# One step of a fused graph-convolution, Mamba and LSTM block: the order of three additions on GpSimd and two activations on ScalarE

## What is computed

```python
h = relu(adj @ layernorm(x) @ gcn_w + gcn_b); h = layernorm(h) * ln_g + ln_b
xz = h @ w_in;  u = silu(conv4(xz[:, :256]) + conv_b);  z = xz[:, 256:]
dbc = u @ w_xp
dt = softplus(dbc[:, :8] @ w_dt + b_dt)          # this line is what the change touches
B, C = dbc[:, 8:24], dbc[:, 24:40]
state[n] = exp(dt * A[n]) * state[n] + dt * B[n] * u      # 16 states n, scan over 8192 tokens
y = sum_n(C[n] * state[n]) + u * D_skip
x1 = x + (y * silu(z)) @ w_out
out = x1 + lstm_part(layernorm(x1))
```

## Time and profile before

| | |
|---|---|
| runs, median of 3 (lowest, highest) | 1579.28 us (1578.86, 1580.91) |
| profiled execution, its own time | 1580.11 us |
| its span in the profile | 1578.3 us |
| TensorE matmul busy | 1504.4 us, 95% |
| VectorE busy | 1360.7 us, 86% |
| GpSimd busy | 1134.1 us, 72% |
| ScalarE busy | 1025.7 us, 65% |
| granted TensorE clock, mean | 0.986 |

### The profile page before, as it was taken

How to read it: one execution, slowest core, us unless ns; L and a number is a source line. 1 busy time by engine, 2 the same in 40 slices (tenths; PEclk the granted TensorE clock), 3 DMA queues, 4 the chain that set the end, 5 groups by cost and what they waited for, 6 DMA issues and landing times. The chain is left out here.

```text
span 1578.3 us, 17939 instructions
## 1 busy us (share of the span) xinstructions
PE 1504.4 (95%) x4976; PEld 768.4 (49%) x4976; DVE 1360.7 (86%) x1617; ACT 1025.7 (65%) x2180; POOL 1134.1 (72%) x542
## 2 busy tenths in 40 slices
PE   7999999999999999999999999999997789999995
PEld 3444434444444444444444444444442235999994
DVE  7405999999999999999999999999999897667998
ACT  3254757666666767676767585757666755777774
POOL 0325989898989898989898898989898883000223
PEclk9999999999999999999999999999998899999998
DMA  9877767777777777676767777777752523000002
GB/s 364 336 244 275 256 230 243 246 252 243 257 244 259 244 238 263 233 260 240 244 238 259 243 249 254 248 252 248 252 190 73 181 74 118 16 0 1 0 0 107
DMA packets 65404, 322.46 MB, mean 204 GB/s; under 512 B 7036, under 2 KB 7088, under 8 KB 32437
## 3 DMA queue, kind: packets, MB, share of 16 engines
q1 hardware_dynamic: 54433, 302.21, 55.0%
q10 hardware_dynamic: 10900, 19.44, 4.2%
HBM read 309.27 MB, written 12.35 MB: 204 GB/s over the span
## 5 line engine op out<-in xcount | busy, mean ns | idle before, releaser
L655 PE MATMUL bank<-ring,xh 128*128 128x512 f32 x2048 | 956.7, 594 | 10.9 <-DVE xh L1296 8.1
L1428 DVE TENSOR_TENSOR_SCAN work<-bank,hstate,work 128x512 f32<-128x512 f32 x512 | 628.8, 1272 | 20.3 <-ACT bank L965 13.0
L655 PEld LDWEIGHTS bank<-ring,xh 128*128 128x128 f32 x2048 | 387.6, 190 | 462.6 <-issue 422.5
L1159 POOL TENSOR_TENSOR work<-work 128x1024 f32<-128x1024 f32 x210 | 495.8, 2361 | 85.5 <-DVE work L1369 77.1
L965 ACT ACTIVATE bank<-work,a_neg 128x512 f32<-128x512 f32 x512 | 344.6, 686 | 250.5 <-DVE work L1428 247.1
L1361 DVE TENSOR_TENSOR work<-work,bank 128x1024 f32<-128x1024 f32 x253 | 307.1, 1219 | 62.2 <-POOL work L1135 54.4
L1369 DVE TENSOR_TENSOR work<-work,bank 128x1024 f32<-128x1024 f32 x168 | 201.8, 1201 | 23.3 <-POOL work L1159 23.3
L541 PE MATMUL bank<-bc_parts,sel 96*128 96x512 bf16 x422 | 161.8, 384 | 23.5 <-DVE work L1361 22.6
L1245 POOL TENSOR_TENSOR work<-work 128x256 f32 x32 | 27.3, 854 | 213.2 <-ACT work L1032 213.2
L536 PE MATMUL bank<-work,w_sb 128*128 128x512 f32 (+2 forms) x352 | 175.3, 594 | 1.3 <-issue 0.8
L1104 POOL TENSOR_TENSOR work<-work 128x1024 f32<-128x1024 f32 x48 | 113.7, 2369 | 18.5 <-ACT work L839 18.4
(11 more groups left out here) (163 smaller groups left out, 1589.7 us busy)
## 6 DMA issues: line engine op xcount, KB each, us to landing
ring<-adj_t SPq DMA_DIRECT2D x256, 1024.0 KB, 5.4
xh<-c_scratch SPq DMA_DIRECT2D x34, 256.0 KB, 3.3
work<-c_scratch ACTq DMA_DIRECT2D x28, 256.0 KB, 5.9
c_two<-c_scratch ACTq DMA_DIRECT2D x28, 256.0 KB, 5.0
xh<-x_rows SPq DMA_DIRECT2D x16, 256.0 KB, 7.2
work<-x_t SPq DMA_DIRECT2D x16, 256.0 KB, 5.3
x_scratch<-work ACTq DMA_DIRECT2D x16, 256.0 KB, 3.6
work<-x_scratch SPq DMA_DIRECT2D x1, 4096.0 KB, 14.6
```

The lines of the kernel that those rows point to most:

```text
L655: last = nc.tensor.matmul(mixed[:, :], xn[:, j, :], a, start=(j == 0), stop=(j == BLK - 1))
L1159: nc.gpsimd.tensor_tensor(out=acc, in0=hc[0] if n == 1 else acc, in1=hc[n % 2], op=ALU.add).then_inc(y_added, 1)
L1428: nc.vector.tensor_tensor_scan(hb[s % 2][:, h, :], da[h], (dbu_late[POOL_DBU.index(s)] if on_pool else dbu[s % 2])[:, h, :], hstate[:, HV ...
```

## The change

On ScalarE the last two of the four activations change places: (1 + e) - 1 now comes third, into wd, and the logarithm fourth, into wc. On GpSimd the first addition is now relu + e, which needs only e. It stands where the remainder stood. Then comes add(11), and only behind it (1 + e) - 1 is taken off, in the new function take_rem. "Low" now waits for that, and no more for add(11). dt is then that result plus the logarithm. In step 16 the first addition goes one slot earlier (slot 11 of the plan, program slot 12), and take_rem stands in slot 12 of the plan. Step 1 has no scan, so both stand together there.

```diff
                         act.wait_ge(one_dt, k)
-                        nc.scalar.activation(wd, wc, ACT.Ln).then_inc(log_dt, 1)
-                        act.wait_ge(log_dt, k)
-                        nc.scalar.activation(wc, wc, ACT.Identity, bias=less_one[:, :]).then_inc(less_dt, 1)
+                        nc.scalar.activation(wd, wc, ACT.Identity, bias=less_one[:, :]).then_inc(less_dt, 1)
+                        act.wait_ge(less_dt, k)
+                        nc.scalar.activation(wc, wc, ACT.Ln).then_inc(log_dt, 1)
...
-                    if s == 12:
-
-                        pool.wait_ge(less_dt, k)
-                        nc.gpsimd.tensor_tensor(out=wb, in0=wc, in1=wb, op=ALU.subtract).then_inc(rem_dt, 1)
+                    if s == (11 if drains(k) else 12):
+
                         pool.wait_ge(pos_dt, HV * k)
-                        pool.wait_ge(rem_dt, k)
-                        nc.gpsimd.tensor_tensor(out=wa, in0=wa, in1=wb, op=ALU.subtract).then_inc(sum_dt, 1)
+                        pool.wait_ge(exp_dt, k)
+                        nc.gpsimd.tensor_tensor(out=wa, in0=wa, in1=wb, op=ALU.add).then_inc(sum_dt, 1)
+                    if s == 12 and not (scan and not drains(k)):
+                        take_rem()
                     if s == 13:
                         pool.wait_ge(mid_rounded, k)
-                        if drains(k):
+                        if scan and drains(k):
                             pool.wait_ge(pool_hc_done, hc_count(cs, 13, True))
-                        elif scan:
-                            pool.wait_ge(y_added, (DS - 1) * cs + 11)
                         else:
-                            pool.wait_ge(sum_dt, k)
+                            pool.wait_ge(rem_dt, k)
...
-                        pool.wait_ge(sum_dt, k)
+                        pool.wait_ge(rem_dt, k)
                         pool.wait_ge(log_dt, k)
-                        nc.gpsimd.tensor_tensor(out=dt[q], in0=wa, in1=wd, op=ALU.add).then_inc(dt_ready, 1)
+                        nc.gpsimd.tensor_tensor(out=dt[q], in0=wa, in1=wc, op=ALU.add).then_inc(dt_ready, 1)
+
+                def take_rem():
+
+                    pool.wait_ge(less_dt, k)
+                    pool.wait_ge(sum_dt, k)
+                    nc.gpsimd.tensor_tensor(out=wa, in0=wa, in1=wd, op=ALU.subtract).then_inc(rem_dt, 1)
...
                     elif scan and s >= 2:
                         add(s - 1)
+                        if pre and s == 12:
+                            take_rem()
```

## The result

The kernel after takes 1592.94 us, median of 4 runs (1591.9 to 1594.93); the kernel before, run beside it, 1580.1 us (4 runs, 1578.86 to 1581.81). The ratio is 1.0076 (95% interval 1.0064 to 1.0088), and the difference 12.8 us. The forecast was 1591.2 us, 11.9 us more than before, in a range of 1586.0 to 1595.5. The profiled execution of the kernel after took 1593.57 us with a span of 1591.7 us, 13.4 us more than the span before; the granted clock is 0.986 of full speed in both. One execution of the kernel before, of the 16 timed beside e5 to e7, took 5588.44 us; it counts as slow and is left out of the ratios there.

What follows compares the result with a forecast made beforehand. Bound: a ring of waits between VectorE and GpSimd, 75.23 us a step, with one through TensorE's `out` close under it. Terms 12.3 + 1.1 - 1.5 = +11.9 us on 1579.28 gave 1591.2 us, range 1586.0 to 1595.5.

Steps and rivals of the forecast that it cites:

- The wait at add(11): GpSimd, scanning steps: add(11) comes one instruction earlier and waits 1.11 us for VectorE's product hc(11).
- The new period: Steps 3 to 15, hc(15) to hc(15): 76.18 us against 75.23, +12.3 us in all.
- VectorE's wait at hc(15): Sign in the profile after: VectorE's wait before hc(15) up from 1.7 to about 2.6 us.
- TensorE's at the spread: Sign in the profile after: TensorE's wait at the spread up from 0.8 to about 1.75 us.
- The 6.0 us that the transfers might have given back: TensorE's weight load waiting for adj data: at most 13 x 0.46 = 6.0 us back, not taken into the forecast.
- Step 2: Scanning step without `out` yet: hc(15) at 210.71 instead of 209.65, +1.1 us.
- Step 1: Step without a scan: earlier relu + e, but the next scan is released by ScalarE's exponential; 0.
- the second ring: hc(15), dbu, TensorE's spread to `out`, hc(11): 59.44 us, slack before; closing, it makes every step pay.
- The rival that the wait is paid once: Steps 3 to 15: TensorE slack between spread and `out` absorbs the delay, no change, 1577.6 us; chance 0.08.
- ScalarE's exchange of two activations: ScalarE's chain of four: same total length, logarithm about 1 us later but covered; cost nothing.
- Step 16, "-1.5 us": GpSimd: first addition falls into its gap behind hc(11), dtu comes 1.56 us earlier; -1.5 us.
- a rival, 1592.7 us: Step 16's gain is lost, held up by TensorE or step 17's loads: 1592.7 us, inside the range; no separate chance.

Runs made afterwards that it cites:

- e5: Kernel after with the subtraction ahead of add(11) again in steps before 16, and dtu behind add(13) in the full steps: 1565.3 us, ratio 0.9897.
- e7: Kernel before with only the new formula and the exchanged activations, additions in their old places in step 16 too: 1580.57 us, ratio 0.9997.
- e1: Kernel after with the subtraction ahead of add(11) again in all scanning steps, step 16 as changed: 1577.15 us, ratio 0.998.
- e2: Kernel after with TensorE's `out` in slot 11 instead of 11.5, not in the drains: 1594.86 us, ratio 1.0092.
- e11: Kernel after with two of TensorE's adjacency products left out in slot 9 of each scanning step up to 15: 1576.93 us, ratio 0.9976.
- e10: Kernel after with GpSimd's hc(0) of step 16 waiting for VectorE's addition of the skip product: 1591.7 us, ratio 1.0061.
- e8: Kernel after with two of TensorE's adjacency products left out in slot 5 of each scanning step up to 15: 1597.33 us, ratio 1.011.
- e9: Kernel before with two of TensorE's adjacency products left out in slot 5 of each scanning step up to 15: 1582.43 us, ratio 1.0006.
- e12: Kernel before with two of TensorE's adjacency products left out in slot 9 of each scanning step up to 15: 1582.94 us, ratio 1.0013.

## Why the prediction was right, and where it was not

**The wait at add(11): right.** Forecast 1.11 us, measured 0.80 to 1.24 us over the 14 steps, and e1 without it loses nothing.

**The new period: right, 76.15 against 76.18 us**, and with it +11.9 against +12.3 us for steps 3 to 15. VectorE's wait at hc(15) came to 2.62 us, TensorE's at the spread to 1.74, VectorE's for `out` stayed at 1.03, as stated. The 6.0 us that the transfers might have given back did not come: from hc(15) to hc(11) it is still 59.50 us in step 7.

**Step 2: right**, +1.05 against +1.1 us. **Step 1** was put at 0; its stretch came 0.42 us earlier, which isn't more than executions differ by.

**Why the second ring closes: the right ring and length, but a wrong link.** The prediction had hc(11) hang on `out`, and took the rest of the way to it as VectorE's own work. In between VectorE's scan waits 0.30 us for ScalarE, and that wait is the one that counts: the ring leaves TensorE at dt's product and goes through ScalarE's activations of the softplus. e2 took `out` out of the way and nothing moved; e11 shortened the queue ahead of dt's product, and the wait at add(11) vanished. The forecast came out because the 59.44 us from hc(15) to hc(11) were measured as a whole, and both links are late by the same amount when TensorE is. That is luck as far as the link goes: had the change also moved `out`, I would have forecast wrongly, as I did for e2. The rival that the wait is paid once rested on slack in TensorE behind its pause. e11 excludes it, for with such slack less work would not have moved hc(11). ScalarE's exchange of two activations was put at nothing since the four together last as before. They do (from L879 to the exponential 6.78 us before, 6.79 after), but by the same reading any activation of this chain that took longer would have been paid in each step.

**Step 16, "-1.5 us": the term that failed.** The gain arose where the prediction put it and as large (1.50 us, in front of dtu), but it did not reach the end: steps 16 and 17 together gave 0.0 us. The prediction named that as a rival, 1592.7 us, and this is what was measured (1592.94). The cause it gave, TensorE or the loads of step 17, is not quite it. Ahead of the softplus the start of step 16 lost 2.31 us, for which the sum had no term. TensorE now pauses 4.32 us at its spread instead of 3.06, and this is its clock in the 16 us around it, before:

```profile
1190.00:1194.00 4.00, 3.55 (x6) 1.03 (x6) 3.77 (x5) 2.17 (x4) 3.71 (x5) 0.60 0.16 60
1194.00:1198.00 4.00, 1.82 (x5) 0.63 (x5) 4.00 (x4) 2.19 (x6) 3.68 (x2) 0.93 0.04 10
```

and after:

```profile
1202.50:1206.50 4.00, 3.56 (x5) 1.35 (x6) 3.53 (x4) 1.56 (x3) 3.71 (x5) 0.50 0.00 0
1206.50:1210.50 4.00, 1.26 (x2) 0.00 (x0) 3.62 (x2) 2.63 (x6) 2.68 (x2) 0.50 0.04 10
```

After the longer pause it stands at 0.50, its 1.2 GHz level, all the way, and what VectorE's addition waits for comes later: that addition now waits 0.85 us for ScalarE instead of 0.23, and starts 0.05 us behind GpSimd's product instead of 0.58 us ahead of it. That it was GpSimd's product that stretched it to 3.38 us is shown by e10. That the lower clock made TensorE's results late fits the rows and was not tested by itself. The rest, 0.8 us gained back in step 17 and 0.9 us lost in the LSTM, is of the size by which such stretches differ with the granted clock.

The time came out 1.7 us above the forecast: 1.5 us are this term, the other 0.2 us the difference of several small ones (steps 3 to 15 gave 0.4 us less than stated, the stretch ahead of step 2 another 0.4 less, the LSTM 0.9 us more).

## What to carry to other kernels

In a pipelined step no engine has to be full for a microsecond to count: look for the ring of waits that closes the step, and for the second longest right under it. Moving one instruction past another on an engine with slack costs the step as soon as its new place asks for something that hangs on the second ring; how much can be read off ahead, as the distance from the step's last event to that input. To find what such an input hangs on, follow the waits ahead of it to the last one, however short: here 0.31 us for ScalarE, and not the 1.03 us for `out` before it. To test it, move that result alone (e2), and take work away from the queue ahead of it at a point where no transfer runs parallel (e11, and e8 for how it fails). And where the last link of the closing ring has an instruction that it doesn't need, as dtu ahead of add(13) here, put it behind: that was worth 14 us, more than the 12.8 us that the change took.

## What the runs showed of the hardware

- **VectorE and GpSimd exclude each other where both read SBUF.** VectorE's 128 x 1024 addition of two SBUF operands takes 1.23 us alone (e10). Started 0.05 us behind GpSimd's product of 2.35 us it takes 3.38 us, about the rest of that product and its own time. In the kernel before it is started during the 1.26 us operation ahead of the product on GpSimd, whose end is at 1193.12 + 1.26 = 1194.38:

```profile
1193.12 1.26 POOL L391 TENSOR_TENSOR work<-work 128x512 f32<-128x512 f32 x1
```

It then ends at 1193.77 + 1.70 = 1195.47, 1.09 us behind that, and it is GpSimd's product that takes 3.33 us. VectorE's hc products, with one operand in a PSUM bank, kept their 1.19 to 1.22 us beside GpSimd's additions. The Trainium skill, page "SBUF — State Buffer", section "🔬 SBUF: two separate sides", has it as an exclusive lock that whoever starts first keeps for the whole instruction; the trace agrees. Half a microsecond of delay changed who was first, and with it who paid.
- **TensorE's clock can fall behind a short pause, and not behind each.** In twelve steps of e8 TensorE pauses 1.62 to 1.94 us in a row of products without gaps. Behind two of these pauses, of 1.83 and 1.89 us, the granted clock was 0.63 and 0.57 over the next 4 us, and the step became 1.8 us longer; behind the other ten, one of 1.94 us among them, it was 1.00. In e9 it was 0.59 behind one of twelve such pauses (1.87 us), and in e12 0.67 behind one of the twelve pauses of 2.00 to 2.04 us at the spread; those steps were 1.1 and 1.3 us longer. Behind the pause of 4.32 us at the start of step 16 it was at 0.50 for over 8 us.
- **GpSimd's neighbours.** A 128 x 1024 operation that needs the result of the one before starts 2.50 us behind it, an independent one 2.32 us. In e11, with one such pair less and no wait at add(11), the steps are 75.06 us, where the kernel before has 75.23.
